# Row sums and variances of the second layer norm moved between VectorE, ScalarE and GpSimd in a gated cross-attention block

## The reference, cut to what matters

```
def layernorm(x): return (x - mean(x)) / sqrt(var(x) + eps)       # over 512 columns

def xattn(logits, features):                                      # logits: layernorm(x), features: ctx
    query = features @ Wq.T + bq;  key = features @ Wk.T + bk     # 256 -> 128
    attention = softmax(query @ key.T, axis=-1)                   # 512 x 512
    return logits @ attention.T

def ffn(x):                                                       # LN with ln_weight, ln_bias
    xn = (x - mean(x)) * rsqrt(var(x) + eps) * ln_weight + ln_bias
    return (xn @ sign(weight).T) * max(abs(weight)) * gamma + beta

x = x + tanh(g_xattn) * xattn(layernorm(x), ctx)                  # x: (4, 512, 512), ctx: (4, 512, 256)
x = x + tanh(g_ffn) * ffn(layernorm(x))
```

## Time and profile before

| what | value |
|---|---|
| median of 3 executions | 136.47 us (136.22 to 136.49) |
| the profiled execution | 135.49 us |
| its span in the trace | 133.7 us |
| granted TensorE clock | 1.00 of full speed (0.999 over the span) |
| instructions in the trace | 1815 |
| DMA | 17.15 MB, mean 128 GB/s |

### The profile page before, as it was taken

One profiled execution on the slowest core, in us unless ns is written; L12 is line 12 of the kernel. 1 busy time (PEld: TensorE's weight loads), 2 busy tenths in 40 slices (PEclk: granted clock), 3 DMA queues, 4 the chain that ended last, 5 costly groups with the idle time before them and its releaser, 6 DMA issues. The chain is left out here.

```text
span 133.7 us, 1815 instructions
## 1 busy us (share of the span) xinstructions
PE 120.2 (90%) x558; PEld 93.6 (70%) x558; DVE 114.4 (86%) x212; ACT 77.5 (58%) x152; POOL 85.3 (64%) x78
## 2 busy tenths in 40 slices
PE   5987999999899987992999999959999999999970
PEld 4525677888587866671878878738888778788660
DVE  1138789989999999899996999999969999999983
ACT  4232999997956972076766970677579715213100
POOL 3005899708327999998432677984416879985670
PEclk9999999999999999999999999999999999999999
DMA  3859995024713411026640420265514202220044
GB/s 79 247 178 403 390 385 202 0 54 147 199 24 135 116 40 72 11 83 230 199 179 14 159 78 5 78 235 159 195 40 153 82 5 78 78 78 0 0 157 157
DMA packets 10648, 17.15 MB, mean 128 GB/s; under 512 B 1808, under 2 KB 2576, under 8 KB 10640
## 3 DMA queue, kind: packets, MB, share of 16 engines
q1 hardware_dynamic: 9920, 17.04, 37.2%
q10 hardware_dynamic: 720, 0.00, 0.3%
HBM read 12.59 MB, written 4.19 MB: 126 GB/s over the span
## 5 line engine op out<-in xcount | busy, mean ns | idle before, releaser
L861 POOL TENSOR_TENSOR xt_lo<-xt_raw,xt_hi 128x512 fp32r<-128x512 f32 x16 | 21.5, 1348 | 13.8 <-ACT xt_hi L508 9.3
L872 POOL TENSOR_TENSOR x<-x,shift 128x512 f32<-128x512 f32 x16 | 20.5, 1287 | 7.6 <-DVE zw L684 7.6
L877 POOL TENSOR_TENSOR x<-x,ffn 128x512 f32<-128x512 f32 x14 | 18.4, 1319 | 2.0 <-DVE ffn L716 2.0
L361 PE MATMUL ps_y<-pt_hi,xt_hi 128*128 128x512 f32 x64 | 18.1, 405 | 1.2 <-issue 1.1
L525 ACT ACTIVATE x_sb<-x_sb,y_bias 128x512 f32<-128x512 f32 x16 | 10.3, 718 | 14.9 <-DVE y_bias L664 14.9
L684 DVE SCALAR_TENSOR_TENSOR zw<-x,mv,ln_w 128x512 f32<-128x512 f32 x16 | 18.4, 1150 | 0.4
L374 PE MATMUL ps_ffn<-w_sign,zt_hi 128*128 128x512 f32 x60 | 17.4, 411 | 0.4 <-DVE ffn L716 0.4
L361 PE MATMUL ps_y<-pt_hi,xt_lo 128*128 128x512 f32 x64 | 17.5, 395 | 0.0
L361 PE MATMUL ps_y<-pt_lo,xt_hi 128*128 128x512 f32 x64 | 17.5, 395 | 0.0
L536 ACT ACTIVATE zt_hi<-ps_turn 128x512 fp32r<-128x512 f32 x16 | 9.5, 595 | 13.6 <-PE ps_turn L328 13.4
L374 PE MATMUL ps_ffn<-w_sign,zt_lo 128*128 128x512 f32 x60 | 16.5, 396 | 0.0
(11 more groups left out here) (149 smaller groups left out, 244.0 us busy)
## 6 DMA issues: line engine op xcount, KB each, us to landing
x_sb<-in_x_dram SPq DMA_DIRECT2D x16, 256.0 KB, 2.6
xt_raw<-in_x_t_dram SPq DMA_DIRECT2D x16, 256.0 KB, 3.1
out_dram<-x SPq DMA_DIRECT2D x15, 256.0 KB, 2.0
ctx_sb<-in_ctx_t_dram SPq DMA_DIRECT2D x8, 256.0 KB, 6.8
w_raw<-in_weight_t_dram SPq DMA_DIRECT2D x4, 256.0 KB, 7.6
ln_w<-in_ln_weight_dram SPq DMA_DIRECT2D x1, 256.0 KB, 7.3
gain<-in_gamma_dram SPq DMA_DIRECT2D x1, 256.0 KB, 7.5
shift<-in_beta_dram SPq DMA_DIRECT2D x1, 256.0 KB, 8.4
```

The costliest lines, as they stand in the source:

```text
L361: mm = pe.matmul(ps_y[t % 2][:, :], lhs[:, t, k, :], rhs[:, k, :], start=(k == 0 and i == 0), stop=(k == KN - 1 and i == 2))
L861: nc.gpsimd.tensor_tensor(xt_lo[:, t, :, :], xt_raw[:, t, :, :], xt_hi[:, t, :, :].bitcast(f32), ALU.subtract).then_inc(xt_lo_done, 1)
L872: nc.gpsimd.tensor_tensor(x1[:, t, :], x1[:, t, :], shift[:, :], ALU.add).then_inc(x1b_done, 1)
L877: nc.gpsimd.tensor_tensor(x1[:, t, :], x1[:, t, :], ffn[:, t % 2, :], ALU.add)\
```

## The change

The sum of x1 over a row now comes from the addition that makes x1 (an accumulator output of line 672). `mean_x1` is one small operation on it. The variance comes from ScalarE: a Square of x1 with the negative mean as bias, whose output goes to a scratch tile and whose sum is kept (`square_x1`). GpSimd turns sums into variances before its power, and also takes over the small operations of the first layer norm (`var_x` and `scale_x` of DVE are gone). The product of `gain` with the weight's scale and the gate is one operation of DVE. `add_shift` overwrites x1 and so now waits for the Square as well.

```
 DVE
-                nc.vector.bn_stats(st2[:, t, :], x1[:, t, :]).then_inc(stat2, 1)
-                dve.drain()
-                nc.vector.bn_aggr(mv2[:, t, :], st2[:, t, :]).then_inc(stat2, 1)
+                nc.vector.tensor_scalar(neg_mean2[:, t:t + 1], sum2[:, t:t + 1], -1.0 / N, None, ALU.mult)\
+                         .then_inc(mean2_done, 1)
 in add_y:
-                                               op0=ALU.mult, op1=ALU.add).then_inc(x1_done, 1)
+                                               op0=ALU.mult, op1=ALU.add,
+                                               accum_out=sum2[:, t:t + 1]).then_inc(x1_done, 1)
 in centre:
-                nc.vector.scalar_tensor_tensor(out=zw[:, t, :], in0=x1[:, t, :], scalar=mv2[:, t, 0:1],
-                                               in1=ln_w[:, :], op0=ALU.subtract, op1=ALU.mult)\
+                nc.vector.scalar_tensor_tensor(out=zw[:, t, :], in0=x1[:, t, :], scalar=neg_mean2[:, t:t + 1],
+                                               in1=ln_w[:, :], op0=ALU.add, op1=ALU.mult)\
 var_both (2 calls a batch), var_x and scale_x (1 call a batch) are removed; in back(0), behind w_scale:
+                    dve.wait_ge(scale_done, 1)
+                    dve.wait_ge(tanh_done, 2)
+                    nc.vector.tensor_scalar(gain[:, :], gain[:, :], w_scale[:, 0:1], tanh_g[:, 1:2],
+                                            ALU.mult, ALU.mult).then_inc(gain_done, 1)
 ACT
+            def square_x1(b, t):
+                act.wait_ge(mean2_done, T * b + t + 1)
+                if T * b + t > 0:
+                    act.wait_ge(square2_done, T * b + t)
+                nc.scalar.activation(unread[:, 2, :], x1[:, t, :], ACT.Square, bias=neg_mean2[:, t:t + 1],
+                                     accum_out=sq_sum2[:, t:t + 1]).then_inc(square2_done, 1)
 bias_x:
-                act.wait_ge(ln1_done, 2 * b + 1)
+                act.wait_ge(ln1_done, 2 * b + 2)
 in the tail:
             for t in range(T):
                 turned_ffn_hi(B - 1, t)
+                square_x1(B - 1, t)
 POOL
 in add_shift:
                 pool.wait_ge(zw_done, T * b + t + 1)
+                pool.wait_ge(square2_done, T * b + t + 1)
+            def scale_x(b):                      # in back where power1(b + 1) stood
+                first = is_first(b)
+                cols = slice(0 if first else HALF, T)
+                if not first:
+                    pool.wait_ge(square1_done, HALF * b)
+                    nc.gpsimd.tensor_scalar(var1[:, :HALF], sq_sum1[:, :HALF], 1.0 / N, EPS, ...)
+                pool.wait_ge(stat1, 2 * T + 2 * HALF * b)
+                nc.gpsimd.tensor_scalar(var1[:, cols], mv1[:, cols, 1], 1.0, EPS, ALU.mult, ALU.add)
+                nc.gpsimd.tensor_tensor(rstd1[:, :], var1[:, :], neg_half[:, :], ALU.pow)
+                if not first:
+                    pool.wait_ge(x1_done, T * b)
+                nc.gpsimd.tensor_tensor(y_scale[:, :], rstd1[:, :], tanh_g[:, 0:1].broadcast_to([P, T]), ALU.mult)
+                nc.gpsimd.tensor_tensor(y_back[:, :], rstd1[:, :], tanh_g[:, 2:3].broadcast_to([P, T]), ALU.mult)
+                if not first:
+                    nc.gpsimd.tensor_tensor(y_bias[:, :HALF], neg_mean1[:, :HALF], y_scale[:, :HALF], ALU.mult)
+                nc.gpsimd.tensor_tensor(y_bias[:, cols], mv1[:, cols, 0], y_back[:, cols], ALU.mult)
             def power2(b, half):
-                pool.wait_ge(stat2, STAT2 * b + (half + 1) * (2 * HALF + 1))
+                pool.wait_ge(square2_done, T * b + (half + 1) * HALF)
+                nc.gpsimd.tensor_scalar(var2[:, cols], sq_sum2[:, cols], (1.0 + EPS) / N, EPS * EPS, ...)
-            nc.gpsimd.tensor_tensor(w_scale[:, :], w_scale[:, :], tanh_g[:, 1:2], ALU.mult)
-            nc.gpsimd.tensor_tensor(gain[:, :], gain[:, :], w_scale[:, 0:1].broadcast_to([P, N]), ALU.mult)
```

More of the change, by code:

```diff
@@ L641, in stats_x @@
                     nc.vector.bn_aggr(mv1[:, t, :], st1[:, t, :]).then_inc(stat1, 1)
[L643 to L656, removed]
-                dve.wait_ge(rstd1_done, b + 1)
-                nc.vector.tensor_scalar(y_scale[:, :], rstd1[:, :], tanh_g[:, 0:1], None, ALU.mult)\
-                         .then_inc(scale1_done, 1)
-                dve.wait_ge(scale1_done, b + 1)
-                if not first:
-                    nc.vector.tensor_tensor(y_bias[:, :HALF], neg_mean1[:, :HALF], y_scale[:, :HALF],
-                                            ALU.mult).then_inc(ln1_done, 1)
-                nc.vector.scalar_tensor_tensor(out=y_bias[:, cols], in0=mv1[:, cols, 0], scalar=-1.0,
-                                               in1=y_scale[:, cols], op0=ALU.mult, op1=ALU.mult)\
-                         .then_inc(ln1_done, 1)
             def add_y(b, t):
@@ L763, in back @@
                 stats_x(b + 1, (3,))
-                var_x(b + 1)
                 scale_ffn(b, 1)
                 turned_ffn_lo(b, 3)
-                scale_x(b + 1)
                 scale_ffn(b, 2)
@@ L836, in _ @@
             stats_x(0, (3,))
-            var_x(0)
             rest_qk(2, 0)
@@ L842, in _ @@
                 turned_prob_lo(0, t)
-            dve.wait_ge(tanh_done, 1)
-            scale_x(0)
             rest_qk(3, 0)
@@ L885, in power2 @@
             def power2(b, half):
-                pool.wait_ge(stat2, STAT2 * b + (half + 1) * (2 * HALF + 1))
+                pool.wait_ge(square2_done, T * b + (half + 1) * HALF)
                 cols = slice(half * HALF, (half + 1) * HALF)
+                nc.gpsimd.tensor_scalar(var2[:, cols], sq_sum2[:, cols], (1.0 + EPS) / N, EPS * EPS,
+                                        ALU.mult, ALU.add).then_inc(var2_done, 1)
+                pool.wait_ge(var2_done, 2 * b + half + 1)
                 nc.gpsimd.tensor_tensor(rstd2[:, cols], var2[:, cols], neg_half[:, cols], ALU.pow)\
@@ L901, in back @@
                 power2(b, 1)
-                power1(b + 1)
+                scale_x(b + 1)
                 split_xt(b + 1, 1)
@@ L940, in _ @@
                     pool.wait_ge(half_done, 1)
-                    power1(0)
+                    pool.wait_ge(tanh_done, 2)
+                    scale_x(0)
             for t in range(HALF, T):
```

60 lines of the change are left out of this document (33 added, 27 removed).

## The result

The changed kernel takes 132.74 us (median; 131.88 to 132.94) where the kernel before took 136.47: ratio 0.972, 95% interval 0.967 to 0.976. In a second comparison on another occasion it was 132.94 against 136.03, ratio 0.979 (0.975 to 0.983).

What follows compares the result with a forecast made beforehand. PE, 90% busy, was taken as the bound, waiting at most 5.8 us for DVE. Terms summed to -2.9 us by batch 3, then tail +1.85: span 132.65; with 1.79, 0.98 and 0.1 for accumulators, 135.5 us, range 133.5 to 138.3.

Steps and rivals of the forecast that it cites:

- 0.98 more again; I add both at the end.: Whole kernel: the median lay 0.98 us above the profiled execution, itself 1.79 above the span; both added to the forecast span.
- Batch 0, -1.65: PE's waits of 0.56 us and, at the start of batch 1's attention, 1.09 us both go: -1.65 us.
- Batch 1, -2.4: PE's transposition at 60.6 against 62.98 us, 1.9 from gain's work leaving POOL; -2.4 contains batch 0's 1.65.
- E: End of POOL's `add_ffn` of tile 1; power2 to there forecast at 6.2 us, PE starting 3.1 us behind it.
- Before it was E+5.6: Kernel before: PE started 5.6 us behind E, whose end `scale_ffn` of tile 3 awaited through two `ffn` buffers.
- Batch 2, 0, and 0.24 for its start: `add_shift` waits for the Square of tile 3, so PE gains 0; a 0.24 us wait at the batch's start goes.
- Batch 3, -0.24: A wait of 0.24 us at the start of batch 3 is lost.
- The tail, +1.85: Last transposition to the end: 10.05 us, was 8.2, because power2 waits for the Square of tile 3: +1.85 us.
- The first: Rival: the one-column mean on DVE also queues behind POOL, 2.8 us more, 138.3 us; chance 0.20.
- the second: Rival: POOL's seven added small instructions cost 0.41 us each, giving 137.6 us; chance 0.13.
- the third: Rival: new collisions, `zw` of tile 1 meeting a POOL instruction, up to 1.25 us; once gives 136.7 us; chance 0.12.
- The fourth: Rival: `zw` of tile 0 finds POOL pausing, PE starts 0.9 us sooner in both batches, 133.7 us; chance 0.13.

Runs made afterwards that it cites:

- the two-column mean: The changed kernel with the mean's TENSOR_SCALAR working on two columns instead of one: 137.24 us, ratio 1.011 to the kernel before.
- Statistics back: Changed kernel with bn_stats and bn_aggr of x1 back on DVE, no accumulator output, no Squares: ratio 0.989 to the kernel before, two executions, 134.09 and 134.82 us.
- four buffers: A buffer for each of the four `ffn` tiles: on the changed kernel 130.48 us, ratio 0.961; on the kernel before 135.77 us, ratio 0.995.
- matmuls of no use: The kernel before with six useless matmuls on PE in front of its 2.5 us wait in batch 1: 135.22 us, ratio 0.997.

## Why the prediction was wrong, step by step

- *PE's idle time is what there is to gain.* Right, but incomplete: I had PE idle for 5.8 us and never asked what happens to PE's clock behind a wait. In two of four traces of the kernel before, and by the mean clock in about half its executions, the wait of 2.52 us in the earlier trace rows was followed by 1.56 us more.
- *"0.98 more again; I add both at the end."* **This step failed.** I took the distance from the profiled execution to the median for a constant. The profiled execution was one without the fall of the clock; the timed ones took 136.22 to 136.49 us, as those with it do (median 136.38; the clocks of these three are not on record). In both traces of the changed kernel, where PE waits 1.45 us, the fall is absent, and it was back when the two-column mean made that wait 2.67 us. Why it comes is not shown. From the start of the scores of batch 1 the gain is 2.0 us against a trace without the fall and 3.6 against one with it (106.85 to 103.25, means of two traces each).
- *How much that step explains.* The forecast missed by 2.8 us, and this step is 0.98 of it. Without it forecast and range would lie 0.98 lower, at 134.5 and 132.5 to 137.3, which holds 132.74. The rest, in the profiled executions: 0.6 for an earlier start, which scatters by more than that from trace to trace, 0.45 in batch 1, 0.35 in the tail, 0.15 in batches 2 and 3, and 0.1 for the accumulators, whose 0.08 us lies in a wait. The terms were nearly all off in the same direction.
- *Batch 0, -1.65.* From the scores of batch 1 to the start of its attention, PE by stretches as above, before and (second fence) after:
```profile
28.40:50.85 22.45, 20.79 (x107) 1.00 0.36 105
```
```profile
27.79:48.13 20.34, 20.34 (x106) 1.00 0.39 116
```
  PE's idle time went from 1.66 us (22.45 less 20.79) to nothing, as said. The stretch shrank by 2.11, since the busy time fell by 0.45 too; that I did not follow up.
- *Batch 1, -2.4.* Measured -2.86. The handover from power2 to E took 5.96 us (6.2 forecast), and E + 3.1 was exact, but E came at 56.43, not 57.5. "The work on gain leaves it and starts earlier; I take 1.9": power2 started 2.74 us earlier (50.47, it was 53.21), of which 0.61 is the start of this execution. Gamma's scaling is 0.8 of the remaining 2.1 us. Statistics back, which has that scaling moved too, starts power2 at 24.04 behind its start and the changed kernel at 22.68, so the lighter DVE gives the other 1.4. So of the 1.9 taken for the work on gain only 0.8 came from it; the total came out right to 0.2 us by luck.
- *"Before it was E+5.6".* As a number right, as a cause wrong. With four buffers the kernel before has E + 5.59 too, so it was not the buffer that tied DVE to E. It was `y_bias`, queued behind the `add_ffn` that ends at E, and DVE's load behind it. With the change the wait for the buffer became the bound, so the way I computed after held, and the four buffers are worth 2.46 us only now.
- *Batch 2, 0, and 0.24 for its start.* Measured -0.63, of which 0.27 is the start: the attention's first product follows the transposition ahead of it by 0.36 us, it was 0.63. E = 75.59 + 7.31, just under my 7.4 to 7.8. That ACT now holds POOL is right, but it is the Square of tile 2, not of tile 3. ACT and POOL there:
```profile
71.86 0.74 ACT L530 ACTIVATE unread<-x,neg_mean 128x512 f32<-128x512 f32 x1
72.84 1.49 POOL L854 TENSOR_TENSOR x<-x,shift 128x512 f32<-128x512 f32 x1 [2.69 <-ACT unread L530]
74.28 1.30 POOL L859 TENSOR_TENSOR x<-x,ffn 128x512 f32<-128x512 f32 x1
75.15 0.19 ACT L530 ACTIVATION_READ_ACCUMULATOR unread<-x,neg_mean 128x1 f32 x1
75.54 1.30 POOL L854 TENSOR_TENSOR x<-x,shift 128x512 f32<-128x512 f32 x1
```
  POOL waits 2.69 us for the first Square. That of tile 3 is read out at 75.34, before POOL's `add_ffn` ends, and its `add_shift` follows without a gap, at the time that I had forecast: the number is near by coincidence of two chains.
- *Batch 3, -0.24.* No gain, 35.44 both times. The wait at its start went (0.35 us from the transposition to the product, it was 0.63), but at 108.19 PE now waits 0.27 us for POOL's `xt_lo`, which I had not forecast.
- *The tail, +1.85.* Measured +1.5. From the end of the last transposition at 121.43: the Square read out at 122.76, power2 done at 123.83, two adds to 126.33, `add_shift` to 128.00, as in my sum, save that copy and Square together took 0.17 us less and `add_shift` waited 0.23 less behind DVE's addition.
- *Not forecast:* 0.23 us ahead of the scores of batch 1. From the first scores (11.02 and 10.64) they come 17.38 us later before and 17.15 after, 17.40 with the first layer norm's small operations back on DVE. One trace with them on POOL, that of four buffers, has 17.48, so the cause is not certain.
- *The rivals.* The first was refuted for one column, and its mechanism is real: with two columns it makes the change slower than nothing. POOL's small instructions take 0.19 to 0.20 us (one took 0.52), 0.27 to a dependent follower, so the second is out. The collisions of the third came (`zw` of tile 1 1.51 and 1.53 us, 0.75 before) and PE did not wait for them. The fourth did not come: `zw` of tile 0 waited in both batches.

## What to carry to other kernels

When a profiled execution is faster than the median, look at the granted clock of the single executions before adding the difference as a constant: a long wait of PE may cost its own length and then a stretch of half clock, and a change that shortens the wait can earn both. A trace of the slower kind shows whether the fall lies there or behind the last matmul, where it cost nothing here. After each change ask again which wait ends last: four buffers moved nothing in the trace of the kernel before and gave 2.5 us with the change. And moving small operations from a full engine to another gives nothing, or costs, if the other's queue then ends the same wait.

## What the runs showed of the hardware

- A DVE TENSOR_SCALAR of one column never queued behind POOL's instruction (136 to 157 ns in 16 instances); the same of two columns took up to 1134 ns.
- The accumulator output on DVE is an instruction of its own, DVE_READ_ACCUMULATOR, 82 ns each (ACT's takes 197). By the Trainium skill (VectorE: DVE Perf Modes, on two Vector instructions with no wait between them) it is two instructions; the trace agrees.
- PE's clock was granted at its lower level behind idle stretches of 2.54, 2.55 and 2.67 us, already inside one of 2.68, and behind one of 1.89 that followed matmuls of no use; it was not behind 2.52 (in two traces), 2.53 (in two) and 1.45. In the four traces of the kernel before it fell in the two that had started early (first scores at 10.2 and 10.0 us) and not in the two others (11.0 and 11.2), but over all traces the start does not decide either: it fell with first scores at 10.9 and 11.1 and did not with 10.6. What decides between 2.53 and 2.54 us, or whether it is the length at all, stays open.
